# Moving work of the normalisations and of the Mamba inputs between VectorE, ScalarE and GpSimd, with the Mamba weights loaded ahead

## What is computed

```python
x = x + layernorm(L(layernorm(x)))      # for each of the 8 layers L
```

```python
xp, z = split(x @ W_in.T)
xc = silu(causal_conv4(xp) + conv_b)
dt_lo, Bm, Cm = split(xc @ W_xp.T)
dt = softplus(dt_lo @ W_dt.T + dt_b)
A = -exp(A_log)
# for each time: h = exp(dt * A) * h + (dt * xc) * Bm;  y = sum_n h * Cm
y = (y + xc * D) * silu(z)
return y @ W_out.T
```

## Time and profile before

| | us |
|---|---|
| median of 3 runs | 4943.62 |
| lowest, highest | 4943.38, 4948.53 |
| the profiled execution | 4947.78 |
| its span in the profile | 4945.9 |
| busy in it: PE | 3930.8 (79%) |
| VectorE | 3734.1 (75%) |
| GpSimd | 2926.6 (59%) |
| ScalarE | 2549.7 (52%) |
| mean granted clock of TensorE | 0.913 |

### The profile page before, as it was taken

The page is one execution under the profiler, slowest core; times in us unless marked ns, Lnnn a source line. Parts: engine busy times, 40 slices in busy tenths (PEclk is TensorE's granted clock), DMA queues, the critical chain, the costliest instruction groups (busy, mean ns, idle before and its releaser), DMA issues. The chain is left out here.

```text
span 4945.9 us, 76468 instructions
## 1 busy us (share of the span) xinstructions
PE 3930.8 (79%) x20245; PEld 2366.6 (48%) x20365; DVE 3734.1 (75%) x6293; ACT 2549.7 (52%) x5336; POOL 2926.6 (59%) x2821
## 2 busy tenths in 40 slices
PE   5888888888578577576979964788888868888884
PEld 3666666666456356365447742333333323333332
DVE  5777777777377378366048857899999889999995
ACT  3555555555344244323246654566666456666662
POOL 2555555555454144143013344899999579999991
PEclk8999999989778878788999987999999989999997
DMA  1000000000000000000000000000000000000000
GB/s 50 9 9 8 9 9 9 8 9 8 16 0 0 21 0 0 12 0 24 0 18 1 1 14 10 0 0 0 0 0 0 8 0 0 0 0 0 0 0 14
DMA packets 90089, 33.37 MB, mean 7 GB/s; under 512 B 78032, under 2 KB 86113, under 8 KB 88929
## 3 DMA queue, kind: packets, MB, share of 16 engines
q1 hardware_dynamic: 89824, 30.17, 2.5%
HBM read 24.89 MB, written 5.24 MB: 6 GB/s over the span
## 5 line engine op out<-in xcount | busy, mean ns | idle before, releaser
L3284 POOL TENSOR_TENSOR dBx<-dtx,b_row 128x1024 f32<-128x1024 f32 x512 | 1219.4, 2382 | 3.9 <-ACT b_row L3250 3.9
L3318 DVE TENSOR_TENSOR_SCAN h<-banks,dBx 128x1024 f32<-128x1024 f32 x512 | 1168.5, 2283 | 19.2 <-ACT banks L3244 19.2
L3202 PE MATMUL banks<-hc,ident 128*128 128x512 f32 x2048 | 964.4, 593 | 0.0
L3244 ACT ACTIVATE banks<-dt,A 128x510 f32<-128x510 f32 x1024 | 661.7, 682 | 4.2 <-DVE h L3318 3.5
L3250 ACT ACTIVATE b_row<-banks 128x512 f32<-128x512 f32 x512 | 305.9, 597 | 574.8 <-PE banks L3186 574.8
L3202 PEld LDWEIGHTS banks<-hc,ident 128*128 128x128 f32 x2048 | 388.5, 190 | 272.3 <-issue 246.8
L3326 DVE TENSOR_TENSOR hc<-h,banks 128x768 f32<-128x768 f32 x512 | 478.6, 935 | 10.8 <-ACT c_row L3255 6.6
L3186 PE MATMUL banks<-bc_lo,selectors 128*128 128x512 bf16 x1024 | 391.3, 382 | 73.8 <-POOL b_row L3273 64.7
L3293 POOL TENSOR_TENSOR hc<-h,c_row 128x256 f32<-128x256 f32 x512 | 376.7, 736 | 55.9 <-ACT c_row L3255 28.7
L3185 PE MATMUL banks<-bc_hm_c,selectors 128*128 128x512 bf16 x506 | 195.1, 385 | 186.0 <-DVE hc L3326 185.6
L3185 PEld LDWEIGHTS banks<-bc_hm_c,selectors 128*128 (+1 forms) x512 | 49.2, 96 | 434.8 <-issue 434.5
(11 more groups left out here) (447 smaller groups left out, 9238.7 us busy)
## 6 DMA issues: line engine op xcount, KB each, us to landing
delta_blocks<-A_turned SPq DMA_DIRECT2D x256, 8.0 KB, 1.5
inv_turned<-delta_blocks SPq DMA_DIRECT2D x256, 8.0 KB, 1.8
blocks<-delta_blocks SPq DMA_DIRECT2D x32, 64.0 KB, 2.1
delta_blocks<-blocks_inv SPq DMA_DIRECT2D x32, 64.0 KB, 1.9
wh<-in_l1f_wh SPq DMA_DIRECT2D x1, 2048.0 KB, 9.0
wqkv<-in_l0f_wqkv SPq DMA_DIRECT2D x2, 768.0 KB, 4.1
residual<-in_x SPq DMA_DIRECT2D x1, 1024.0 KB, 4.7
wv<-in_l0a_wv SPq DMA_DIRECT2D x1, 1024.0 KB, 7.3
```

The source lines that it names most:

```text
L3202: i = nc.tensor.matmul(k.bank[e], k.ident[:], hc[:, s, e, :], start=False, stop=False)
L3244: i = nc.scalar.activation(a3[:, :, 1:], d3[:, :, 1:], ACT.Exp, scale=mem["A"][:, e, bass.ds(n, 1)])
L3284: nc.gpsimd.tensor_tensor(dBx[:, s % NS], dtx[:, :, bass.ds(c * SCH, SCH)], across(bsb[:, s % NS, :], SE), ALU.mult).then_inc(q["dbx_ready ...
L3318: v.tensor_tensor_scan(flat(h[:, s % NS]), flat(k.banks[:, at:at + SE, :]), flat(dBx[:, s]), 0.0, ALU.mult, ALU.add).then_inc(q["scanned"], 1)
```

## The change

In the normalisation between blocks the sums X + H of groups 0 and 2 go from GpSimd to VectorE, and the second-round applies of groups 2 and 3 from ScalarE to VectorE (new semaphore `applied_late`). VectorE's order changes with them, and ScalarE's copies to HT come behind its applies.

```diff
@@ add_and_normalise, GpSimd
                 powers(0, 2)
-                add(0)
                 powers(0, 3)
                 add(1)
                 powers(1, 0)
-                add(2)
                 powers(1, 1)
                 add(3)
@@ VectorE
                 def statistics(r, g):
-                    if r == 1:
-                        dve.wait_ge(added, g + 1)
+                    if r == 1 and g % 2 == 1:
+                        dve.wait_ge(added, g // 2 + 1)
...
+                def add(g):
+                    dve.wait_ge(applied, g + 1)
+                    nc.vector.tensor_tensor(k.X[:, cols(g), :], k.X[:, cols(g), :], k.H[:, cols(g), :], ALU.add)
+                    dve.drain()
+
+                def apply(g):
+                    dve.drain()
+                    for t in tiles(g):
+                        i = nc.vector.tensor_scalar(k.H[:, t, :], k.X[:, t, :], rstd[:, 1, t:t + 1], shift[:, 1, t:t + 1],
+                                                    ALU.mult, ALU.add)
+                    i.then_inc(applied_late, 1)
...
                 shift_of(0, 2)
+                add(0)
+                statistics(1, 0)
                 shift_of(0, 3)
-                statistics(1, 0)
                 statistics(1, 1)
                 shift_of(1, 0)
+                add(2)
                 statistics(1, 2)
                 shift_of(1, 1)
                 statistics(1, 3)
                 shift_of(1, 2)
+                apply(2)
                 shift_of(1, 3)
+                apply(3)
@@ ScalarE
                 apply(1, 0)
-                for g in range(1, NG):
-                    apply(1, g)
-                    copy_turned(g - 1)
-                copy_turned(NG - 1)
+                apply(1, 1)
+                for g in range(NG):
+                    copy_turned(g)
@@ PE
-                    pe.wait_ge(applied, NG + g + 1)
+                    if g < 2:
+                        pe.wait_ge(applied, NG + g + 1)
+                    else:
+                        pe.wait_ge(applied_late, g - 1)
```

```diff
@@ bi_mamba
-        normalise(k, src=k.H, affine=affine[:, 0])
         with Part(k) as p:
-            mem = mamba_memories(p)
+            mem = mamba_memories(k, p)
+            normalise(k, src=k.H, affine=affine[:, 0], meanwhile=lambda sp: load_mamba_weights(k, sp, mem))
...
+def load_mamba_weights(k, sp, m):
+    for n in (1, 2):
+        for dst, src in m[n]["loads"]:
+            sp.dma_start(dst[:], src).then_inc(m["loaded"], 16)
+    sp.dma_start(m["self"][:], k.dram["l3a_sel"]).then_inc(m["loaded"], 16)
@@ mamba_inputs: PE, ScalarE, VectorE
-                pe.wait_ge(q["loaded"], 112)
+                pe.wait_ge(mem["loaded"], 208)
```

```diff
@@ ScalarE
                 exps(1)
+                logs(0)
+                logs(1)
                 high(3)
                 exps(2)
-                logs(0)
-                logs(1)
+                exps(3)
                 logs(2)
-                exps(3)
                 logs(3)
@@ GpSimd: one_plus and scaled_x are gone
-                split(0)
-                split(1)
-                one_plus(0)
...
-                scaled_x(2)
+                for c in range(SNC):
+                    split(c)
@@ VectorE
                 def positive_part(c):
                     for e in range(SE):
                         dve.wait_ge(q["exped"], 2 * c + e + 1)
+                        v.tensor_scalar_add(u[:, e, cols(c)], en[:, e, cols(c)], 1.0).then_inc(q["u_ready"], 1)
+                    for e in range(SE):
                         v.tensor_scalar(dt[:, e, cols(c)], bank_of(c, e), cw[:, e, 5:6], 0.0, ALU.add, ALU.max).then_inc(q["dt_read"], 1)
+                    dve.drain()
                     for e in range(SE):
-                        dve.wait_ge(q["u_ready"], 2 * c + e + 1)
                         x = en[:, e, cols(c)]
...
@@ softplus
                         x = dt[:, e, cols(c)]
-                        v.tensor_tensor(x, x, en[:, e, cols(c)], ALU.add).then_inc(q["dt_done"], 1)
-
-                def skip_part(c):
+                        v.tensor_tensor(x, x, en[:, e, cols(c)], ALU.add)
+                    dve.drain()
                     for e in range(SE):
-                        if c < SNC - 1:
-                            dve.wait_ge(q["dtx_done"], 2 * c + e + 1)
+                        v.tensor_tensor(dtx[:, e, cols(c)], dt[:, e, cols(c)], xc[:, e, cols(c)], ALU.mult)
+                    dve.wait_ge(q["bc"], 4 * c + 4)
+                    dve.drain()
+                    for e in range(SE):
                         v.tensor_scalar(xc[:, e, cols(c)], xc[:, e, cols(c)], cw[:, e, 6:7], None, ALU.mult)
@@ VectorE's order
                 positive_part(1)
+                softplus(0)
+                softplus(1)
                 split(3)
                 positive_part(2)
-                softplus(0)
-                softplus(1)
+                positive_part(3)
                 softplus(2)
-                skip_part(0)
-                skip_part(1)
-                positive_part(3)
-                skip_part(2)
                 softplus(3)
-                dve.drain()
-                for e in range(SE):
-                    v.tensor_tensor(dtx[:, e, cols(3)], dt[:, e, cols(3)], xc[:, e, cols(3)], ALU.mult)
-                dve.drain()
-                skip_part(3)
```

More of the change, by code:

```diff
@@ L138, in add_and_normalise @@
         var, power, shifts = p.sem("var"), p.sem("power"), p.sem("shifts")
-        applied, added, turned = p.sem("applied"), p.sem("added"), p.sem("turned")
+        applied, applied_late = p.sem("applied"), p.sem("applied_late")
+        added, turned = p.sem("added"), p.sem("turned")
         tiles = lambda g: range(g * G, (g + 1) * G)
@@ L2830, with mamba_memories @@
 CPAD = 3
-def mamba_memories(p):
+def mamba_memories(k, p):
     m = {}
@@ L2842, in mamba_memories @@
         m[n] = p.sb("bc_" + n, [P, B * T], BF16)
-    m["A"] = p.sb("A", [P, SE, SN])
     m["sel"] = p.sb("selectors", [P, 3, SN], BF16)
     m["self"] = p.sb("selectors_f32", [P, 3, SN])
-    m["cw"] = p.sb("conv_and_biases", [P, SE, 7])
-    m["wout"] = p.sb("w_out", [P, SE, D])
+    R = D // 16
+    shapes = dict(win=[P, 4 * P], conv=[P, SE, 7], wxp=[P, SE, 3 * P + R], wdt=[R, 2 * P], alog=[P, SE, SN], wout=[P, SE, D])
+    m["loaded"] = p.sem("weights_loaded")
+    for n in (1, 2):
+        w = {x: p.sb(f"{x}_{n}", shape) for x, shape in shapes.items()}
+        m[n] = dict(win=w["win"], cw=w["conv"], wxp=w["wxp"], wdt=w["wdt"], A=w["alog"], wout=w["wout"])
+        m[n]["loads"] = [(w[x], k.dram[f"l3a_{x}{n}"]) for x in shapes]
     return m
@@ L2856, in mamba_inputs @@
     xp, xc, sz, dt, dtx = (mem[n] for n in ("xp", "xc", "sz", "dt", "dtx"))
-    cw = mem["cw"]
+    mem.update(mem[m])
+    cw, win, wxp, wdt = (mem[n] for n in ("cw", "win", "wxp", "wdt"))
     with Part(k) as p:
-        win, wxp = p.sb("w_in", [P, 4 * P]), p.sb("w_xp", [P, SE, 3 * P + R])
-        wdt = p.sb("w_dt", [R, 2 * P])
         dtlo = p.sb("dt_low", [R, B * T])
@@ L2865, in mamba_inputs @@
         r1 = p.sb("rest", [P, SCH])
-        names = ("loaded", "src_ready", "xproj", "xp_out", "zproj", "z_out", "conved", "xc_ready", "bc", "hi_ready", "split_read",
-                 "hm_copied", "lo_done", "rest", "dtlo_ready", "dtp", "exped", "dt_read", "u_ready", "logged", "dt_done",
-                 "dtx_done", "a_ready")
+        names = ("src_ready", "xproj", "xp_out", "zproj", "z_out", "conved", "xc_ready", "bc", "hi_ready", "split_read",
+                 "hm_copied", "lo_done", "rest", "dtlo_ready", "dtp", "exped", "dt_read", "u_ready", "logged", "a_ready")
         q = {n: p.sem(n) for n in names}
@@ L2879, in mamba_inputs @@
         with nc.Block() as block:
[L2880 to L2884, removed]
             @block.tensor
@@ L2981, in logs @@
                         fn(dtx[:, e, cols(c)], u[:, e, cols(c)], ACT.Ln).then_inc(q["logged"], 1)
-                act.wait_ge(q["loaded"], 112)
+                act.wait_ge(mem["loaded"], 208)
                 copy_x(0)
@@ L3021, in split @@
                     tt(mem["lo"][:, cols(c)], r1[:], mid[:], ALU.subtract).then_inc(q["lo_done"], 1)
-                def one_plus(c):
-                    for e in range(SE):
[L3025 to L3031, removed]
-                split(0)
-                split(1)
-                one_plus(0)
-                split(2)
-                one_plus(1)
-                split(3)
-                one_plus(2)
-                scaled_x(0)
-                scaled_x(1)
-                one_plus(3)
-                scaled_x(2)
+                for c in range(SNC):
+                    split(c)
             @block.vector
@@ L3105, in _ @@
                 v.memset(xp[:, :, 0:CPAD], 0.0).then_inc(q["src_ready"], 1)
-                dve.wait_ge(q["loaded"], 112)
+                dve.wait_ge(mem["loaded"], 208)
                 v.tensor_copy(mem["sel"][:], mem["self"][:])
```

1 line of the change is left out of this document (removed).

## The result

The changed kernel takes 4884.7 us by the median of four executions (4875.01 to 4889.52) beside 4943.5 (4933.74 to 4948.53): a ratio of 0.9884, 95% interval 0.9865 to 0.9902. Two more comparisons gave 0.9887 [0.9866, 0.9907] and 0.9894 [0.9877, 0.9911].

A forecast was written before the change was run, and what follows sets the result against it. A chain over engines, not one engine, was taken to bound the normalisation. Normalisations 29.4, weights 7.1 + 2.8 and tails 2 x 2.3 sum to 43.9 us off 4943.6, giving 4899.7 us; range 4889 to 4916.

The forecast's parts named there:

- Sum: Whole kernel: gains in normalisations, weight loads and input-stage tails add to 43.9 us, median 4899.7, range 4889 to 4916.
- The normalisation: Seven normalisations between blocks: last copy at 18.9 us instead of 23.08, 4.2 us less each, 29.4 in all.
- Rival 1: Normalisations: GpSimd powers and VectorE operations exclude each other; last copy at 20.5, only 18.2 us gained, total 4911; chance 0.12.
- The weights: Mamba input stages: weights loaded earlier, in the affine normalisation, end the wait for loads; 7.1 us gained in first, 2.8 second.
- The tail: Input stages from the first exponentials: fewer GpSimd collisions outweigh added VectorE work; 2.3 us gained each, bounds 0 and 3.8.
- Rival 2: Input-stage tail gains 0 as collisions with GpSimd's splits return, and the first Mamba's clock falls; total 4906; chance 0.08.
- Rival 3: Mamba scans slow down through changed SBUF placement; 0.086 us per step cancels the gain, 0.15 gives 4977; chance 0.04.
- Rival 4: Whole kernel unchanged: loads still late, or the last group not the end of the normalisation; chance 0.03.

## Why the prediction was wrong, point by point

- **The step that failed: "Sum", with its range.** It set every unedited stretch at its time of before, and let only "a few us of the runs' spread" into the range. The attention block's 729 us were taken as fixed because nothing in it was edited. It begins 3.8 us earlier, and its mean course is 10 us shorter (719.3 for 729.0), at a granted clock of 0.83 in six profiles of seven where it was 0.80 to 0.82. The edited stretches themselves gave 43.4 us for a forecast of 43.9, so nearly all of the miss lies in a term that the sum put at nothing. I had read rows of the granted clock for the gap in the earlier trace rows and asked what the clock does in the stage behind it; I didn't ask it of the blocks behind the other normalisations.
- **The normalisation: right, a little too large.** 26.8 us in seven where 29.4 was forecast. The sixth ends at 19.57 and not 18.9. The power beside a sum costs 0.44 us and not 0.2, twice, and beside the applies nothing: the 14 such powers are the 6.1 us by which the group of the earlier trace rows grew, from 56.7 to 62.8. Both GpSimd sums also begin later, by this and because the first round's statistics end at 6.5 us and not at 6.13, and hold VectorE until 2925.6 and 2930.0, 9.3 and 13.6 us behind the first statistics, where I had 8.7 and 12.8.
- **Rival 1, a mutual hold: no.** It wanted powers of 2 us and an end at 20.5. VectorE was never held by a power. The Trainium skill (SBUF — State Buffer, section "SBUF: two separate sides") has the lock on the ports that VectorE and GpSimd share exclusive for the whole instruction, for the one that starts first. The trace agrees for GpSimd's sums (0.64 us for 0.17) and not for its powers, beside which the four applies kept their 1.12 us. That a power loses 0.44 us when it begins 0.1 us into a VectorE sum of 0.69 shows contention the other way, though less than the 0.59 us that were left of the sum.
- **The weights: right.** 7.0 and 3.0 us in the run with them alone, forecast 7.1 and 2.8. Over the 1.5 us ahead of the first projection the clock was 0.83: 0.50 up to 2954.7, inside the transposes, and 1.00 from there. The copies are 0.79 and 0.86 us apart (2956.90, 2957.69, 2958.55), so it didn't fall again. The 13 loads are issued from 2936.23 to 2941.91, and nothing waits for them.
- **The tail: the right size, a little low.** 3.0 and 2.3 us alone, forecast 2.3 each; on top of the weights 3.0 and 3.7, with the spread of a us or two in the second stage. The stage from PE's start takes 74.9, forecast 75.6. Rival 2 is out: of 9.1 + 7.4 + 5.1 us of VectorE work 7.3 went, and GpSimd's splits didn't bring them back.
- **Rival 3, longer scans: no.** 818.07 us after and 818.33 before in the first Mamba.
- **Rival 4, no effect: no.** No engine waits for a load, and the sixth normalisation ends 3.5 us earlier.

What stays open: by what steps the clock takes its course in the attention block; why six edited normalisations alone are 8 us short of their due, and the changed kernel with the old first one 7 us. In both profiles the block behind the second normalisation took 230.35 us, 6.6 more than in the profile of before; the same block ran from 223.8 to 230.9 over all profiles, so this points the same way and shows nothing. Nor was it tried whether another start makes the attention block shorter still.

## What to carry to other kernels

An edit that moves the start of a later block by a few us can change that block's time by more than the edit's own worth, where the block runs at a mix of TensorE's two clock levels. Sum the edited stretches for the forecast, and give each long block of that kind behind the edit a spread of its own, in both directions (here 10 us on 729), in the range. And before a surplus is put down to the edit, put the old order back in front of that block, or shift it by dead work, and see whether the surplus goes. Read in the profile how far the block really moved: here a memset of 1.76 us moved it by nothing.

## What the runs showed of the hardware that was not expected

- TensorE's granted clock took different courses over the same instructions, and some came again to within 0.1 us: over the 19 profiles the part with the 624 matmuls took 114.1 us twice, 122.0 to 122.1 twelve times, and 115.7, 118.3, 121.7, 125.4 and 125.6 once each. The changed kernel has three of these lengths in its three profiles (114.1, 115.7 and 122.0).
- Single executions of one kernel spread: 4879.29 to 4906.96 us with one memset, 4875.01 to 4907.27 for the changed kernel. The longer ones mostly have the lower mean clock: with one memset 0.925 in the shortest and 0.918 and 0.916 in the two longest.
- A power of GpSimd that begins inside a VectorE sum takes 1.45 us for 1.02, and the sum keeps its 0.69.
- In the first normalisation GpSimd's memset comes 4.0 us behind VectorE's first statistics (1302.07 and 1298.12), in the sixth 0.9 (2917.29 and 2916.36), in the others 0.2 to 1.4. A memset of 1.76 us on VectorE ahead of the first statistics there costs nothing (22.1 us from end to start for 22.2, and 26.0 for 26.0).
